# Expert shares carried in sorted rows, gathers that add to the residual, and products four heads at a time

## The chip, the core and the metric

The kernel runs on one core of a Trainium2 chip. The metric is the device time of one execution in microseconds (us), the median over several runs. The core has TensorE (PE; its weight loads are listed as PEld), VectorE (DVE), ScalarE (ACT) and GpSimd (POOL); SyncE (SP) issues most transfers, GpSimd issues the indirect ones. Each engine works through its own list of instructions in order, and semaphores order the engines among one another. SBUF is the memory the engines work in, PSUM the banks TensorE writes.

## What is computed

A decoder of two layers over x of 64 sequences of 64 positions and 256 channels, in float32; each sublayer normalises x and adds its result to it:

```python
# layer 0: gated linear attention of 16 heads, a recurrence over the context, experts
x = x + linear_attention(layernorm(x))
x = x + recurrence(k=layernorm(x), v=ctx, w, u)
h = layernorm(x)
top, index = top_2(h @ router_weight.T + router_bias)      # of 8 experts
share = softmax(top)                                       # two shares per token
x = x + sum over the two choices of share * expert(h)
# layer 1: attention D (windowed), cross attention E, attention F with a modulated MLP M
x = x + attention_D(layernorm(x))
q = (layernorm(x) @ Wq + bq), k, v = ctx @ Wk + bk, ctx @ Wv + bv    # 16 heads of 16
# scores between the HEADS of one token: 16 x 16 per token
x = x + softmax_g(q[h] . k[g]) v[g] @ Wo + bo
x = x + attention_F(...) ; x = x + mlp_M(...)
```

(The factor of the expert sum is taken into the shares: the kernel's expert outputs are twice the real ones, and its shares are halved.)

## The kernel before, in words

There are 4096 tokens, 32 tiles of 128 (one token per partition); x stays in SBUF as `x_sb` [128, 32, 256] from start to end. Three stages follow one another with a barrier between: linear attention (to 1480 us), `recurrence_and_experts` (to about 1935 us) and `layer_one`.

**Recurrence and router.** Eight blocks of four tiles go through ten steps (`STEPS`), with three blocks in work: one is being normalised and transposed, one scanned, one routed. On the routed block VectorE adds the recurrence's result (`residual`), takes statistics, and after TensorE's router product picks the two largest experts (`choose`, L1431 to L1441), ranks tokens within an expert and turns that into row numbers (`place`, L1458 to L1468). ScalarE computes the exponential of the gap of the two scores (`odds`, L1281). VectorE computes the two shares (`settle`, L1446 to L1451) in the next step, into `wts` [128, 32, 2]. GpSimd scatters the normalised rows `xh`, 256 floats each, to `sorted_rows` in HBM, grouped by expert: one indirect DMA per tile and choice (L1031), 64 in all, spread over the next step of its list. At the end VectorE makes a table of 39 tiles of 256 sorted rows, which expert each belongs to and where it starts (`tile_table`, L1487 to L1516), and SP fills the end of each expert's rows with zeros (L927) before any row is loaded.

**Experts.** For each of 39 tiles SP loads 256 rows (L945, four buffers `hs`) and 1 MB of gate and up weights (L951, three buffers), TensorE transposes the rows (L1198), multiplies with gate and up (L1211) and, after the activation, with down (L1225). ScalarE copies the transposes (`hT_out`), applies tanh, adds the bias to the up half (`up_out`) and copies the product (`aT_out`); VectorE makes the low parts (`rows_low`, L1560), the gate (L1571), L1577, the product (L1583) and the result (`result`, L1590, into two buffers `ys`), GpSimd clamps (L1072) and makes the low part (L1076). SP stores the results to `sorted_outs` (L956), in sorted order. In each engine's loop these pieces stand in an order that is written out by hand, several tiles apart.

**Layer one.** Here too the order is written by hand: `iterate` runs a counter i and calls, for each engine, a list of (stage, piece); a piece works on tile i - FIRST[stage]. FIRST is G=-2, Dn=-1, D=0, Dt=1, En=1, E=2, Et=3, F=4, Ft=5, M=7, Md=8, so eight to ten tiles are in work, each in another stage. What matters here:

- G, on GpSimd (`gather`): a copy of the tile's row numbers, two tiny instructions that act as fences (L1810 to L1814), and two indirect DMAs (L1816) that fetch the outputs of both choices into `got0` and `got1`.
- Dn, on VectorE (`combine`, L2221): x += share * got, twice; then the statistics of D.
- E: q to SBUF (L2080), then GpSimd multiplies (`products_qk`, L1797): 16 instructions, one per head, of 16 x 16 elements. VectorE sums four heads at a time (`et_scores`, L2295), subtracts the maximum (L2300, L2302), ScalarE exponentiates, VectorE divides (`et_weights`, L2307 to L2311). GpSimd multiplies the weights with the values (`products_av`, L1804), again 16 instructions, and VectorE sums (`et_values`, L2319). Both sets go through one buffer `prod`. TensorE transposes and projects the result (L1854, L1849) and VectorE adds it to x (`et_x`, L2325).
- F and M: `arguments` (L2266, L2269), `statistics` (L2232), `divide` (L2279, L2282), `f_x2lo` (L2341), `ft_gm_lo` (L2336), the MLP's silu (`m_hidden`, L2358, L2361), `m_x` (L2367). The first piece in GpSimd's list is F's power (L1787), so it stands behind the gathers of the iteration before.

TensorE's list in layer one is ("M", m_half(0)), D's and E's transposes, ..., ("F", f_zT), ("M", m_half(1)), ..., ("Md", m_down), ("Et", et_aT), ("Et", et_wo), ("F", f_s), and m_half waits until the silu has left the bank `GA`.

## Time and profile before

| | us |
|---|---|
| median of 3 runs | 3035.04 |
| lowest and highest | 3031.03, 3040.39 |
| the profiled execution, its own time | 3033.89 |
| its span in the trace | 3032.2 |
| TensorE busy | 2750.8 |
| VectorE busy | 2487.2 |
| ScalarE busy | 1954.2 |
| GpSimd busy | 2111.9 |

The profile is of one execution. The page gives busy time, a chain of waits followed back from the end and the costliest groups of instructions; the trace behind it gives every instruction with start and duration, and for idle time what ended it. A start is in us from the start of the span. "x16" is a run of sixteen alike instructions merged into one row. A duration includes the tail of a pipelined instruction, so the next can start before it is over; the steps from start to start tell what one costs in a row.

### The profile page before, as it was taken

How to read it: one execution, taken by the hardware profiler on the slowest of the kernel's cores; microseconds unless marked ns; L12 is line 12 of the kernel's file. 1: busy time of each engine (PE TensorE's matmuls, PEld its weight loads, DVE VectorE, ACT ScalarE, POOL GpSimd, SP SyncE). 2: the span in 40 equal slices, each digit the busy share in tenths (PEclk: the TensorE clock that was granted, in tenths of full speed). 3: DMA queues.
4: the chain of work that ended last, by engine and by line, in shares of the span. 5: the costliest groups of instructions: out<-in, count | busy, mean ns of one | idle time of the engine just before them, and what ended most of it. 6: DMA issues, size and time to landing. Idle time of an engine off the chain costs nothing. (4 is left out here: it accounts for less than half of the span.)

```text
span 3032.2 us, 68140 instructions
## 1 busy us (share of the span) xinstructions
PE 2750.8 (91%) x22096; PEld 2295.9 (76%) x22128; DVE 2487.2 (82%) x5452; ACT 1954.2 (64%) x4120; POOL 2111.9 (70%) x2651
## 2 busy tenths in 40 slices
PE   6999999999999999999788499667999999999978
PEld 3888888888888888888555299535777777777767
DVE  6888888888888888888599577468899898989863
ACT  5888878778787877878444155346666666666642
POOL 5897666666666666666468544369888989898870
PEclk9999999999999999999899699768999999999989
DMA  4555444444444444444444399600000000000000
GB/s 144 172 193 169 133 143 139 144 135 146 137 131 153 131 143 132 155 131 128 142 152 146 134 337 333 207 15 18 20 19 27 21 25 24 22 24 22 21 5 11
DMA packets 185881, 340.09 MB, mean 112 GB/s; under 512 B 40668, under 2 KB 104037, under 8 KB 178936
## 3 DMA queue, kind: packets, MB, share of 16 engines
q1 hardware_dynamic: 179448, 319.55, 32.6%
q0 software_dynamic: 6144, 16.79, 1.8%
q8 instruction: 169, 2.77, 0.4%
q14 instruction: 120, 0.98, 0.1%
HBM read 264.68 MB, written 63.19 MB: 108 GB/s over the span
## 5 line engine op out<-in xcount | busy, mean ns | idle before, releaser
L1804 POOL TENSOR_TENSOR l_prod<-l_sco,l_kv 128x256 f32<-128x256 f32 x512 | 369.5, 760 | 36.4 <-DVE l_sco L2311 36.4
L1797 POOL TENSOR_TENSOR l_prod<-l_q,l_kv 128x256 f32<-128x256 f32 x512 | 358.9, 743 | 47.3 <-DVE l_att L2319 47.3
L718 DVE SCALAR_TENSOR_TENSOR a_cq<-a_PQ,a_taps,a_cq 128x504 f32<-128x504 f32 (+2 forms) x384 | 281.7, 734 | 72.7 <-ACT a_cq L584 63.6
L718 DVE SCALAR_TENSOR_TENSOR a_ck<-a_PK,a_taps,a_ck 128x504 f32<-128x504 f32 (+2 forms) x384 | 280.6, 731 | 9.7 <-ACT a_ck L584 0.5
L342 POOL TENSOR_TENSOR a_tq<-a_cq,a_tq 128x512 f32<-128x512 f32 x128 | 165.9, 1296 | 131.2 <-ACT a_tq L590 131.1
L329 POOL TENSOR_TENSOR a_hrs<-a_hve,a_neghalf 128x8 f32<-128x8 f32 x128 | 209.6, 1638 | 25.7 <-DVE a_hve L735 25.2
L485 PE MATMUL a_Y<-a_wo,a_og_parts 128*128 128x256 f32 x1536 | 205.9, 284 | 5.0 <-POOL a_og_parts L336 5.0
L412 PEld LDWEIGHTS a_X<-a_wv,a_xb 128*128 128x128 f32 x1536 | 200.0, 188 | 12.1 <-issue 1.2
L342 POOL TENSOR_TENSOR a_tk<-a_ck,a_tk 128x512 f32<-128x512 f32 x128 | 163.6, 1278 | 62.8 <-ACT a_tk L590 62.8
L412 PE MATMUL a_PQ<-a_x_hi,a_wqk 128*128 (+1 forms) x512 | 194.1, 420 | 12.6 <-issue 11.9
L412 PE MATMUL a_X<-a_wv,a_xb 128*128 128x256 f32 x1536 | 204.2, 282 | 0.8 <-DMA a_xb<-a_x_lo 0.8
L603 ACT ACTIVATE a_hk<-a_PK,a_lncol 128x512 f32<-128x512 f32 x128 | 99.9, 781 | 154.6 <-PE a_PK L504 154.6
L485 PEld LDWEIGHTS a_Y<-a_wo,a_og_parts 128*128 128x128 f32 x1536 | 194.7, 192 | 6.0 <-issue 5.9
L597 ACT ACTIVATE a_nq<-a_TQ,a_hnb,a_hrs 128x128 f32<-128x128 f32 x512 | 192.5, 463 | 1.5 <-POOL a_hnb L332 1.0
L597 ACT ACTIVATE a_nk<-a_TK,a_hnb,a_hrs 128x128 f32<-128x128 f32 x512 | 191.5, 457 | 0.0
L412 PE MATMUL a_X<-a_x_hi,a_wg 128*128 (+1 forms) x512 | 183.5, 399 | 2.3 <-DVE a_og L743 2.3
L412 PE MATMUL a_PK<-a_x_hi,a_wqk 128*128 (+1 forms) x512 | 182.6, 397 | 0.0
L336 POOL TENSOR_TENSOR a_og_parts<-a_og,a_og_parts 128x512 fp32r<-128x512 f32 x128 | 166.7, 1302 | 17.6 <-ACT a_og_parts L610 17.6
L584 ACT ACTIVATE a_cq<-a_PQ,a_taps 128x512 f32<-128x512 f32 x128 | 99.9, 780 | 100.0 <-PE a_PQ L412 100.0
L325 POOL TENSOR_TENSOR a_hm<-a_hst 128x8 f32<-128x8 f32 x128 | 26.7, 209 | 191.9 <-DVE a_hst L724 191.9
L772 DVE TENSOR_TENSOR_SCAN a_em<-a_dr,a_dm 128x256 f32<-128x256 f32 x128 | 160.0, 1250 | 0.0
L2319 DVE TENSOR_REDUCE l_att<-l_prod 128x64 f32<-128x1024 f32 x128 | 151.7, 1206 | 8.2 <-POOL l_prod L1804 8.0
(398 smaller groups left out, 8380.6 us busy)
## 6 DMA issues: line engine op xcount, KB each, us to landing
a_wqk<-qk_parts SPq DMA_DIRECT2D x112, 512.0 KB, 3.4
m_wgu<-gate_up_parts SPq DMA_DIRECT2D x39, 1024.0 KB, 8.1
a_wv<-v_parts SPq DMA_DIRECT2D x56, 512.0 KB, 3.8
a_wg<-g_parts SPq DMA_DIRECT2D x112, 256.0 KB, 3.3
a_wo<-o_parts SPq DMA_DIRECT2D x112, 256.0 KB, 2.9
a_dr<-decays SPq DMA_DIRECT2D x256, 64.0 KB, 2.6
m_hs<-sorted_rows SPq DMA_DIRECT2D x39, 256.0 KB, 7.1
sorted_outs<-m_ys SPq DMA_DIRECT2D x39, 256.0 KB, 7.5
```

What stands on the lines that cost most here:

```text
L329: nc.gpsimd.tensor_tensor(out=hrs[q][:], in0=hve[q][:], in1=neghalf[:], op=ALU.pow).then_inc(s_hrstd, 1)
L336: nc.gpsimd.tensor_tensor(out=og_parts[q][:, 1, :], in0=og[q][:], in1=og_parts[q][:, 0, :].bitcast(F32), op=ALU.subtract).then_inc(og_lo, 1)
L342: nc.gpsimd.tensor_tensor(out=t[i][p][:], in0=c[i][p][:], in1=t[i][p][:], op=ALU.mult).then_inc(s_silu, 1)
L412: last = nc.tensor.matmul(out, lhs(i, k), rhs(j, k), start=at_pass == PASSES[0], stop=at_pass == PASSES[-1])
L485: last = nc.tensor.matmul(Y[:, j, :], og_parts[p][:, i, j * P:(j + 1) * P], wo[p][:, w, :], start=first and j % 2 == 0 and k == 0, stop=Tr ...
L584: nc.scalar.activation(c[i][p][:], PB[i][:], ACT.Identity, bias=taps[p][:, bias:bias + 1], scale=taps[p][:, tap + KW - 1:tap + KW]).then_i ...
L597: nc.scalar.activation(nrm[i][q][:, j, :], TB[i][:, j, :], ACT.Identity, bias=hnb[q][:, k:k + 1], scale=hrs[q][:, k:k + 1]).then_inc(s_nor ...
L718: nc.vector.scalar_tensor_tensor(out=acc, in0=src, scalar=taps[p][:, tap + k:tap + k + 1], in1=acc, op0=ALU.mult, op1=ALU.add).then_inc(s_ ...
L772: nc.vector.tensor_tensor_scan(out=flat(em[q]), data0=flat(dr[q]), data1=flat(dm[q]), initial=0.0, op0=ALU.mult, op1=ALU.add).then_inc(s_e ...
L1797: nc.gpsimd.tensor_tensor(out=prod[:, h], in0=qv[:, h:h + 1, :].to_broadcast([P, H, HD]), in1=kk, op=ALU.mult).then_inc(S("E_pqk"), 1)
L1804: nc.gpsimd.tensor_tensor(out=prod[:, h], in0=sco[:, h:h + 1, :].to_broadcast([P, HD, H]), in1=vv, op=ALU.mult).then_inc(S("E_pav"), 1)
L2319: nc.vector.reduce_sum(att[:].rearrange("p (h d) -> p h d", d=HD)[:, 4 * k:4 * k + 4, :], prod[:, 4 * k:4 * k + 4], axis=AX).then_inc(S("E ...
```

## The change

Rows that are scattered are three floats wider: they carry the number of the token's first expert, the share of the second choice (`SHARE`) and what the first has more (`MORE`). In the expert stage VectorE compares the first number with the tile's expert and so gets each row's share (`first_choice`, `shares`), and ScalarE multiplies the result with it (`weigh`) before it is stored; `ys` has three buffers and the store comes one step later. The buffer `wts` is gone. In layer one the gathers add straight to `x_sb` in the DMA, the first choice in a new stage G0 (FIRST -3) and the second in G, which waits for the first; `combine`, the copies and the fences are gone. The products of cross attention are issued for four heads at a time.

```diff
...
     I2 = 2 * D
+    FIRST_EXPERT, MORE, SHARE, WIDE = D, D + 1, D + 2, D + 3
...
-        zeros, ends = sb("zeros", [P, D]), sb("ends", [P, E], mybir.dt.int32)
+        zeros, ends = sb("zeros", [P, WIDE]), sb("ends", [P, E], mybir.dt.int32)
...
-        xh = some(2, "xh", [P, BT, D])
+        xh, w0 = some(2, "xh", [P, BT, WIDE]), sb("w0", [P, BT])
...
-            hs = own_some(4, "hs", [P, 2, D])
+            hs = own_some(4, "hs", [P, 2, WIDE])
+            pick, w_of = own_some(2, "pick", [P, 2]), own_some(8, "w_of", [P, 2])
...
+            aT, ys = own_some(2, "aT", [P, 2, DC, ROWS], F32R), own_some(3, "ys", [P, 2, D])
...
-            LOADS, STORES = 4, 2
+            LOADS, STORES = 4, 3
...
-                             zeros[:].unsqueeze(1).to_broadcast([P, 2, D])).then_inc(S("filled"), 16)
+                             zeros[:].unsqueeze(1).to_broadcast([P, 2, WIDE])).then_inc(S("filled"), 16)
...
@@ -941,6 +943,7 @@
                 def load(i):
                     if i >= LOADS:
                         sp.wait_ge(S("x_hT"), i - LOADS + 1)
+                        sp.wait_ge(S("x_share"), i - LOADS + 1)
                     at = sp.value_load(where_i[0:1, i:i + 1], min_val=0, max_val=E * ROOM)
                     sp.dma_start(hs[i % LOADS][:], rows[bass.ds(at, ROWS), :].rearrange("(h p) d -> p h d", p=P)).then_inc(S(f"x_in{i % LOADS}"), 16)
...
                 def store(i):
-                    sp.wait_ge(S("x_y"), i + 1)
+                    sp.wait_ge(S("x_ys"), 2 * i + 2)
...
                         load_weights(i)
-                for i in range(-3, N + 1):
-                    if i >= 1:
-                        store(i - 1)
+                for i in range(-3, N + 2):
+                    if i >= 2:
...
                 def scatter(b, part=slice(0, 2 * BT)):
                     pool.wait_ge(S("slot"), b + 1)
                     pool.wait_ge(S("xh"), 4 * b + 4)
+                    pool.wait_ge(S("carried"), 3 * b + 3)
                     for j, k in [divmod(n, 2) for n in range(2 * BT)][part]:
...
-                        nc.scalar.activation(out[:, j, :], x_sb[:, b * BT + j, :], ACT.Identity, bias=nm[k][:, j:j + 1],
+                        nc.scalar.activation(out[:, j, 0:D], x_sb[:, b * BT + j, :], ACT.Identity, bias=nm[k][:, j:j + 1],
...
-                for i in range(-3, N):
+                def weigh(i):
+                    act.wait_ge(S("x_share"), i + 1)
+                    act.wait_ge(S("x_y"), i + 1)
+                    for h in range(2):
+                        nc.scalar.activation(ys[i % STORES][:, h, :], ys[i % STORES][:, h, :], ACT.Identity,
+                                             scale=w_of[i % 8][:, h:h + 1]).then_inc(S("x_ys"), 1)
+
+                for i in range(-3, N + 1):
                     if i + 3 < N:
                         hT_out(i + 3)
                     if 0 <= i + 1 < N:
@@ -1367,6 +1378,8 @@
                     if 0 <= i + 2 < N:
                         tanh(i + 2)
                         up_out(i + 2)
+                    if i >= 1:
+                        weigh(i - 1)
...
                     nc.vector.tensor_copy(ixf[:, b * BT:(b + 1) * BT, :], ix8[:, :, 0:2]).then_inc(S("ixf"), 1)
+                    nc.vector.tensor_copy(xh[b % 2][:, :, FIRST_EXPERT], ix8[:, :, 0]).then_inc(S("carried"), 1)
...
                     dve.wait_ge(S("odds"), b + 1)
                     nc.vector.tensor_scalar(te[:, 2, :], te[:, 1, :], 1.0, 2.0, ALU.add, ALU.mult).then_inc(S("sum2"), 1)
                     dve.wait_ge(S("sum2"), b + 1)
-                    own_w = wts[:, b * BT:(b + 1) * BT, :]
-                    nc.vector.reciprocal(own_w[:, :, 0], te[:, 2, :]).then_inc(S("w0"), 1)
+                    nc.vector.reciprocal(w0[:], te[:, 2, :]).then_inc(S("w0"), 1)
                     dve.wait_ge(S("w0"), b + 1)
-                    nc.vector.tensor_tensor(out=own_w[:, :, 1], in0=own_w[:, :, 0], in1=te[:, 1, :], op=ALU.mult).then_inc(S("w1"), 1)
+                    share, more = xh[b % 2][:, :, SHARE], xh[b % 2][:, :, MORE]
+                    nc.vector.tensor_tensor(out=share, in0=w0[:], in1=te[:, 1, :], op=ALU.mult).then_inc(S("carried"), 1)
+                    dve.wait_ge(S("carried"), 3 * b + 2)
+                    nc.vector.tensor_tensor(out=more, in0=w0[:], in1=share, op=ALU.subtract).then_inc(S("carried"), 1)
...
                         weights_low(y)
-                    if r:
-                        settle(r - 1)
...
                     if r is not None:
                         place(r)
+                        settle(r)
                 tile_table()
-                settle(BLOCKS - 1)
...
+                def first_choice(i):
+                    dve.wait_ge(S(f"x_in{i % LOADS}"), 16 * (i // LOADS + 1))
+                    row = hs[i % LOADS]
+                    nc.vector.scalar_tensor_tensor(out=pick[i % 2][:], in0=row[:, :, FIRST_EXPERT], scalar=who[:, i:i + 1],
+                                                   in1=row[:, :, MORE], op0=ALU.is_equal, op1=ALU.mult).then_inc(S("x_pick"), 1)
+
+                def shares(i):
+                    dve.wait_ge(S("x_pick"), i + 1)
+                    if i >= 8:
+                        dve.wait_ge(S("x_ys"), 2 * (i - 8) + 2)
+                    nc.vector.tensor_tensor(out=w_of[i % 8][:], in0=pick[i % 2][:], in1=hs[i % LOADS][:, :, SHARE],
+                                            op=ALU.add).then_inc(S("x_share"), 1)
...
                     if i + 3 < N:
+                        first_choice(i + 3)
                         rows_low(i + 3)
+                        shares(i + 3)
...
-    FIRST = dict(G=-2, Dn=-1, D=0, Dt=1, En=1, E=2, Et=3, F=4, Ft=5, M=7, Md=8)
+    FIRST = dict(G0=-3, G=-2, Dn=-1, D=0, Dt=1, En=1, E=2, Et=3, F=4, Ft=5, M=7, Md=8)
...
-        got = [sb(f"got{k}", [P, D]) for k in range(2)]
-        of_tile, ready = sb("of_tile", [P, 2], mybir.dt.uint32), sb("ready", [P, 1])
...
-                    sp.wait_ge(S("E_pav"), H * (t - 2))
+                    sp.wait_ge(S("E_pav"), 4 * (t - 2))
...
@@ -1793,32 +1820,31 @@
                 wait_if(pool, S("E_att"), 4 * t)
                 qv = q[:].rearrange("p (h d) -> p h d", d=HD)
                 kk = kv[t % 3][:, 0, :].rearrange("p (g d) -> p g d", d=HD)
-                for h in range(H):
-                    nc.gpsimd.tensor_tensor(out=prod[:, h], in0=qv[:, h:h + 1, :].to_broadcast([P, H, HD]), in1=kk,
-                                            op=ALU.mult).then_inc(S("E_pqk"), 1)
+                for k in range(4):
+                    heads = slice(4 * k, 4 * k + 4)
+                    nc.gpsimd.tensor_tensor(out=prod[:, heads], in0=qv[:, heads, :].unsqueeze(2).to_broadcast([P, 4, H, HD]),
+                                            in1=kk.unsqueeze(1).to_broadcast([P, 4, H, HD]), op=ALU.mult).then_inc(S("E_pqk"), 1)
             def products_av(t):
                 pool.wait_ge(S("E_w"), t + 1)
                 vv = kv[t % 3][:, 1, :].rearrange("p (d g) -> p d g", d=HD)
-                for h in range(H):
-                    nc.gpsimd.tensor_tensor(out=prod[:, h], in0=sco[:, h:h + 1, :].to_broadcast([P, HD, H]), in1=vv,
-                                            op=ALU.mult).then_inc(S("E_pav"), 1)
-
-            def gather(t):
-                wait_if(pool, S("G_ready"), 2 * t)
-                wait_if(pool, S("G_x"), 2 * t)
-                nc.gpsimd.tensor_tensor(out=ready[:], in0=neghalf[:, 0:1], in1=neghalf[:, 0:1], op=ALU.mult).then_inc(S("G_ready"), 1)
-                nc.gpsimd.tensor_copy(of_tile[:], slots[:, tile(t), :].rearrange("p t k -> p (t k)")).then_inc(S("G_at"), 1)
-                pool.wait_ge(S("G_ready"), 2 * t + 1)
-                pool.wait_ge(S("G_at"), t + 1)
-                nc.gpsimd.tensor_tensor(out=ready[:], in0=neghalf[:, 0:1], in1=neghalf[:, 0:1], op=ALU.mult).then_inc(S("G_ready"), 1)
-                for k in range(2):
-                    nc.gpsimd.indirect_dma_start(got[k][:], None, outs[:, :],
-                                                 bass.IndirectOffsetOnAxis(ap=of_tile[:, k:k + 1], axis=0)).then_inc(S(f"G_in{k}"), 16)
+                for k in range(4):
+                    heads = slice(4 * k, 4 * k + 4)
+                    nc.gpsimd.tensor_tensor(out=prod[:, heads], in0=sco[:, heads, :].unsqueeze(2).to_broadcast([P, 4, HD, H]),
+                                            in1=vv.unsqueeze(1).to_broadcast([P, 4, HD, H]), op=ALU.mult).then_inc(S("E_pav"), 1)
+
+            def gather(k):
+
+                def piece(t):
+                    if k:
+                        pool.wait_ge(S("G_in0"), 16 * t + 16)
+                    nc.gpsimd.indirect_dma_start(x_sb[:, t, :], None, outs[:, :], bass.IndirectOffsetOnAxis(ap=slots[:, t, k:k + 1], axis=0),
+                                                 compute_op=ALU.add).then_inc(S(f"G_in{k}"), 16)
+                return piece
             pool.wait_ge(S("masked"), 4)
             iterate(pool, [("F", power("F", 2)), ("Et", products_av), ("Dn", power("D", 1)), ("En", power("E", 1)), ("E", products_qk),
-                           ("G", gather)])
+                           ("G", gather(1)), ("G0", gather(0))])
...
-
-            def combine(t):
-                for k in range(2):
-                    dve.wait_ge(S(f"G_in{k}"), 16 * t + 16)
-                    if k:
-                        dve.wait_ge(S("G_x"), 2 * t + 1)
-                    nc.vector.scalar_tensor_tensor(out=row(t), in0=got[k][:], scalar=wts[:, tile(t), k:k + 1].rearrange("p t k -> p (t k)"),
-                                                   in1=row(t), op0=ALU.mult, op1=ALU.add).then_inc(S("G_x"), 1)
...
-                    wait_if(dve, S("E_pav"), H * t)
-                    dve.wait_ge(S("E_pqk"), H * t + 4 * k + 4)
+                    wait_if(dve, S("E_pav"), 4 * t)
+                    dve.wait_ge(S("E_pqk"), 4 * t + k + 1)
...
                     wait_if(dve, S("E_aTp"), t)
-                    dve.wait_ge(S("E_pav"), H * t + 4 * k + 4)
+                    dve.wait_ge(S("E_pav"), 4 * t + k + 1)
...
-                          ("M", m_hidden(0)), ("D", d_rope), ("Dn", combine), ("Et", et_values(0)), ("Ft", divide("F", MI)),
-                          ("Dn", statistics("D", "G_x", 2)), ("F", f_x2lo), ("Dt", d_x), ("M", m_hidden(1)),
+                          ("M", m_hidden(0)), ("D", d_rope), ("Et", et_values(0)), ("Ft", divide("F", MI)),
+                          ("Dn", statistics("D", "G_in1", 16)), ("F", f_x2lo), ("Dt", d_x), ("M", m_hidden(1)),
...
-        wts = ctx.enter_context(nc.sbuf_tensor("wts", [P, TILES, 2], F32))
-        rows = nc.dram_tensor("sorted_rows", (8 * (TOK + 2 * P) + 2 * P, D), F32, kind="Internal").ap()
+        rows = nc.dram_tensor("sorted_rows", (8 * (TOK + 2 * P) + 2 * P, D + 3), F32, kind="Internal").ap()
...
```

## Rows read from the trace of the kernel before

**Rows 1.** The page's chain of waits, shares by engine.
```profile
DVE 11%; POOL 10%; PE 8%; issue 6%; ACT 1%; DVEq 0%; POOLq 0%; ACTq 0%
```

**Rows 2.** Busy time by stretch: PE, PEld, DVE, ACT, POOL; clock, DMA share, GB/s.
```profile
1750.00:1930.00 180.00, 177.95 (x1504) 177.75 (x1502) 134.35 (x228) 97.81 (x189) 87.79 (x114) 1.00 0.94 314
2300.00:2830.00 530.00, 498.15 (x4384) 400.18 (x4401) 479.11 (x984) 329.04 (x824) 475.77 (x708) 1.00 0.08 24
```

**Rows 3.** Timeline, VectorE, a tile: start, us, operation, count, idle before.
```profile
2515.25 0.42 DVE L2325 TENSOR_TENSOR x_sb<-l_EB,x_sb 128x256 f32<-128x256 f32 x1 [1.60 <-PE l_EB L1849]
2524.80 0.42 DVE L2282 TENSOR_TENSOR l_oD<-l_EB,l_recD 128x256 f32<-128x256 f32 x1
2526.22 0.68 DVE L2358 SCALAR_TENSOR_TENSOR l_hid<-l_hid,l_GA 128x512 f32<-128x512 f32 x1
2529.32 1.72 DVE L2221 SCALAR_TENSOR_TENSOR x_sb<-l_got,wts,x_sb 128x256 f32<-128x256 f32 x2
2545.24 0.42 DVE L2325 TENSOR_TENSOR x_sb<-l_EB,x_sb 128x256 f32<-128x256 f32 x1 [1.58 <-PE l_EB L1849]
```

**Rows 4.** Timeline, TensorE in the same tile.
```profile
2527.04 0.95 PE L2019 MATMUL l_GA<-l_x,l_win 128*128 128x256 f32 x6
```

**Rows 5.** Timeline, GpSimd's products in the first and the last tiles.
```profile
1998.18 10.94 POOL L1797 TENSOR_TENSOR l_prod<-l_q,l_kv 128x256 f32<-128x256 f32 x16
2013.13 11.28 POOL L1804 TENSOR_TENSOR l_prod<-l_sco,l_kv 128x256 f32<-128x256 f32 x16 [0.65 <-DVE l_sco L2311]
2025.83 16.01 POOL L1797 TENSOR_TENSOR l_prod<-l_q,l_kv 128x256 f32<-128x256 f32 x16 [0.38 <-DVE l_att L2319]
2058.95 10.93 POOL L1797 TENSOR_TENSOR l_prod<-l_q,l_kv 128x256 f32<-128x256 f32 x16 [0.47 <-DVE l_att L2319]
2088.63 11.01 POOL L1797 TENSOR_TENSOR l_prod<-l_q,l_kv 128x256 f32<-128x256 f32 x16 [2.12 <-DVE l_att L2319]
...
2900.04 11.02 POOL L1797 TENSOR_TENSOR l_prod<-l_q,l_kv 128x256 f32<-128x256 f32 x16 [2.01 <-DVE l_att L2319]
2931.40 11.00 POOL L1797 TENSOR_TENSOR l_prod<-l_q,l_kv 128x256 f32<-128x256 f32 x16 [5.41 <-DVE l_att L2319]
2946.37 11.20 POOL L1804 TENSOR_TENSOR l_prod<-l_sco,l_kv 128x256 f32<-128x256 f32 x16 [3.31 <-DVE l_sco L2311]
```

**Rows 6.** Groups of GpSimd in the recurrence: busy us, mean ns, idle before.
```profile
L1025 POOL TENSOR_TENSOR m_fv<-m_fk,m_vt 128x1024 f32<-128x1024 f32 x8 | 18.8, 2351 | 0.2 <-ACT m_fk L1271 0.2
L1018 POOL TENSOR_TENSOR m_ev<-m_eh,m_vt 128x1024 f32<-128x1024 f32 x8 | 17.4, 2178 | 10.7 <-ACT m_eh L1266 10.7
```

**Rows 7.** The gathers' tile: time from issue to landing.
```profile
DMA to landing us min/median/max: 2.7/2.8/7.3
```

**Rows 8.** Timeline, VectorE at the start of layer one.
```profile
1948.56 0.48 DVE L2221 SCALAR_TENSOR_TENSOR x_sb<-l_got,wts,x_sb 128x256 f32<-128x256 f32 x1 [0.84 <-DMA l_got<-sorted_outs,l_of_tile]
```

**Rows 9.** Transposes of the experts' rows: ns min/median/max, first and last start.
```profile
L1198 PE MATMUL m_TV<-ident,m_hs x156: 270/272/476, 1738.2 to 1917.6; 128*128 128x128 f32 x156
```

**Rows 10.** Timeline, VectorE's gate of two expert tiles.
```profile
1751.34 0.87 DVE L1571 TENSOR_SCALAR m_gp<-m_TK,m_bias_of 128x256 f32<-128x256 f32 x2
1755.61 0.87 DVE L1571 TENSOR_SCALAR m_gp<-m_TK,m_bias_of 128x256 f32<-128x256 f32 x2
```

**Rows 11.** Timeline of the recurrence: a scatter on GpSimd, the last slot numbers.
```profile
1628.57 0.98 POOL L1031 DMA_INDIRECT sorted_rows<-m_xh,m_sent_to  x1 [3.02 <-DVE m_sent_to L1468]
...
1721.20 0.17 DVE L1468 CAST m_sent_to<-m_row_of 128x8 uint32<-128x8 f32 x1
```

**Rows 12.** Timeline, ScalarE, four normalisations in a row.
```profile
1656.61 2.07 ACT L1258 ACTIVATE m_xn<-x_sb,m_nm,m_rs 128x256 f32<-128x256 f32 x4 [2.93 <-POOL m_nm L1004]
```

**Rows 13.** DMA queues from 1760 to 1920 us: packets, MB, share.
```profile
q1 hardware_dynamic: 22718, 51.95, 97.4%
```

**Rows 14.** Timeline, VectorE, a four-element instruction of the recurrence.
```profile
1622.98 2.60 DVE L1431 TENSOR_TENSOR m_te<-m_mx 128x4 f32<-128x4 f32 x1
```

**Rows 15.** One line's instructions: duration ns min/median/max, first and last start.
```profile
L2341 DVE TENSOR_TENSOR l_x<-l_x2f,l_x x32: 412/416/2843, 2051.0 to 2975.9; 128x256 fp32r<-128x256 f32 x32
```

## Prediction of the time, made before the changed kernel ran

> **What bounds the kernel now.** I read the page first, for its chain of waits, then the windows for the three stretches that the change touches, then the timelines of one tile of layer one, engine by engine. The chain of waits is shared out over VectorE, GpSimd and TensorE [rows 1], so no engine bounds alone. In the steady part of layer one TensorE is busy 498.15 of 530 us, VectorE 479.11 and GpSimd 475.77, at the full granted clock (1.00, 2.4 GHz) [rows 2]. There the order of the queues decides, and the timelines show the loop. A period is the step between two residual additions of cross attention on VectorE (L2325): 2515.25 to 2545.24, 29.99 us [rows 3]. Both start after an idle gap of 1.60 and 1.58 us that ended with TensorE's product (L1849), so VectorE has slack there. From 2515.25 VectorE works without a gap to the silu (L2358, ends 2526.90), 11.65 us; D's division (L2282) at 2524.80 is in it [rows 3]. TensorE's next gate product (L2019) starts at 2527.04, 0.14 us after the silu frees its bank [rows 4], and TensorE then runs through its in-order list to the product that VectorE waits for at 2545.24 [rows 3], 18.2 us. 11.65 + 0.14 + 18.2 = 29.99: this loop, half VectorE and half TensorE, sets the period. The two weighted additions of the expert outputs (L2221, 1.72 us at 2529.32) [rows 3] are behind the silu and ahead of the gap, in the part of VectorE's list with 1.6 us of slack.
>
> At the ends of layer one it is otherwise. In the first three tiles GpSimd runs its two sets of 16 products nearly back to back, with idle gaps of 0.65, 0.38 and 0.47 us, and the loop is 2025.83 - 1998.18 = 27.65, then 33.12, then 29.68 us, the last of them ending in a wait of 2.12 us for VectorE. In the last tiles the sets stand alone on the path with only softmax and reductions between [rows 5].
>
> **The products.** Sets of 16 instructions of 256 elements take 10.94 and 11.28 us where little disturbs them [rows 5], some 0.69 each, 2.77 us for four heads. One instruction of 1024 elements on GpSimd takes 2.351 or 2.178 us [rows 6]. So a set of four costs 8.7 to 9.4 us; I take the middle, 9.06, a saving of 1.9 and 2.2 us per set. These rows have plain operands, not ones spread over heads; bounds are no saving and the full 8.7. VectorE's reductions work on four heads at a time already and wait for the same data.
> - First tiles: loop 1 saves both sets, 4.1 us. Loop 2 as much, 4.2 (its set of 16.01 us [rows 5] holds a stall beside VectorE's split of weights that stays). Loop 3, which ends in VectorE's wait, some 2.5, and the next 0.8. Together -11.6 (-6 to -14).
> - Steady tiles: neither set is in the loop above. 0 (-1 to +1).
> - Last tiles: the sets at 2931.40 and 2946.37 are wholly on the path: 11.00 + 11.20 - 18.12 = 4.1. The one at 2900.04 holds back F's power behind it in the queue: 2.0. Of the loop before I count 1.5 and of the values' set in between 1.0. Together -8.6 (-4 to -11).
>
> **The gathers.** Both additions leave VectorE: 1.72 us per tile less, but in the slack, so the gap at L2325 grows from 1.60 to 3.3 us and the period stays. GpSimd loses three small instructions and keeps two gathers. In a steady tile the second gather is a whole period behind the first, so its wait is met, and its landing has over 10 us before D's statistics. An accumulating gather isn't in the trace; a plain one lands in 2.7 to 7.3 us [rows 7]. At the start of layer one it costs: now both first gathers fly together beside the weight loads, and the second addition runs at 1948.56 for 0.48 us [rows 8]. After, the second is issued only when the first has landed. One landing more is 2.8 to 7.3 us [rows 7]; I take 6, as the weight loads fill the queues, less 2 for the addition, the three small instructions and the spacing of the two: +4 (+2 to +7). Behind that wait on GpSimd stands D's power, which needs the same data anyway.
>
> **The experts.** The transposes of 39 tiles start from 1738.2 to 1917.6 [rows 9], 4.72 us a tile, with TensorE busy 177.95 of 180 us [rows 2]: it is the bound. Added per tile are two VectorE instructions on 2 elements, in the loop gate, tanh, up, clamp, product, rows, gate. Where TensorE doesn't hold it that loop takes 1755.61 - 1751.34 = 4.27 us [rows 10]; two small ones (an estimate of 0.17 us each, the length of the small cast [rows 11]) make it 4.6, under 4.72. ScalarE gains two activations on 256 elements; four such take 2.07 [rows 12], so 1.04 a tile, and it is busy 54% [rows 2]. They fit where it now waits for the transposes. SP's store now waits for the scaling, with the loads of rows and weights queued behind it; it comes one step later and has a third buffer, so by then the scaling is done. The loads wait in addition for the shares, which follow the transposes at once. Rows of 1036 bytes are 1.2% more of a sixth of the bytes, and the hardware queue is at 97.4% [rows 13], still under. With so little room I add 2 us for jitter (0 to 8), and 1.1 for the last tile's scaling, ahead of its store.
>
> **The recurrence.** Shares are settled right after the slots, and each scatter waits for them. The settling waits for ScalarE's exponential of the same step, which is a router's step old by then; behind it on VectorE stand the next step's statistics. GpSimd already waits for the slot numbers (3.02 us before a scatter [rows 11]), so a scatter and the power queued behind it come some 0.4 us later, and VectorE has two more instructions of some 0.17 us. 0.35 x 8 = 2.8. After the last slots (cast at 1721.20 [rows 11]) the settling stands ahead of the table that the loads wait for: 0.7. Together +3.5 (+1 to +6).
>
> **Sum.** 3.5 + 2 + 1.1 + 4 - 11.6 + 0 - 8.6 = -9.6 us. The profiled execution took 3033.89 us (span 3032.2), so 3024.3; the median of the runs is 1.15 above it: 3025.5. All low ends together give -22, all high ends +13. A measurement of this kernel can tell 0.3%, 9.1 us, from no change: the border is 3026, so this forecast is as likely just over it as under.
>
> **Rivals.**
> - Each tile gets shorter by what VectorE loses. For it: VectorE leads the chain of waits with 11% [rows 1] and is busy 90%. Against it: the gap of 1.60 us in every period [rows 3]. If the 1.72 us count in the 27 tiles from the fourth to the end of D: 3025.5 - 46 = 2979.
> - The products don't get shorter, as the operands spread over four heads cost per element what they cost now. Nothing in the trace shows the form. The 20.2 us of both ends go, but 3 for the small instructions ahead of F's power: 3025.5 + 17 = 3043.
> - Slower, by longer waits between VectorE and GpSimd. A VectorE instruction of 4 elements took 2.60 us at 1622.98 [rows 14], in the stretch where GpSimd runs instructions of 1024 elements, and L2341 took up to 2.84, with a median of 0.42 [rows 15]. Both read two SBUF tensors. L2341 and L2336 are such, both between silu and L2325, beside products that now last 2.3 us. Two full waits are 4.7 us against 3.3 of slack; as all tiles keep the same phase it is all of them or none. It decides from 3.3 us on; at 1.0 over in 27 tiles: 3025.5 + 27 = 3052. Against it: the median of L2341 shows no wait at all in most of its 32 runs [rows 15].
> - Wide rows are moved as if they had 2048 bytes. A sixth of 4.7 us more DMA time a tile, 0.78, less 0.12 of room, in 39 tiles: 3025.5 + 26 = 3051. Nothing speaks for it but that no row of the trace has such a size with such starts.
>
> On the third of these the Trainium skill speaks against the change. Its page "SBUF — State Buffer", section "SBUF: two separate sides", says that VectorE with two SBUF inputs and GpSimd take a shared port pair for a whole instruction, and the loser is blocked until the end. By that rule the wait grows with the length of a product, fourfold. The trace agrees in the row at 1622.98; the 2.84 us beside products of 0.69 is longer than the rule gives.
>
> **How the numbers follow.** Forecast 0.64, tiles shorter 0.15, products no shorter 0.08, port waits 0.08, wide rows 0.05. The predicted time is the forecast's, 3025. All of its ends together give 3013 and 3048, which hardly meet; with the spread of the runs themselves (3031.03 to 3040.39) its own range is 3008 to 3043. Up to 3052 the three others come in, and the first rival (0.15) and the tails stay out; the low end gets 2 us more for a period that shrinks a little. Over 0.3% faster: half of the forecast and the first rival, 0.32 + 0.15 = 0.47. Slower by over 0.3%: port waits 0.08, wide rows 0.05, 0.03 from the products' case and 0.02 from the forecast's tail, 0.18. Within: the rest, 0.35.
>
> **What would show it.** In the timeline of GpSimd a set of four near 9.1 us; the step between two L2325 (now a later line) still 30.0 us, with the idle gap before it at 3.3; no VectorE line for gathers, D's statistics of the first tile near 1953; the experts' transposes still 4.72 us apart; the first three loops of products shorter by 4, 4 and 2.5 us. A period under 29.5 or over 30.3 us would make the prediction wrong, as 27 tiles multiply it; so would experts' tiles 0.3 us longer, or a landing of an accumulating gather of over 10 us.

## The result and the profile after

The changed kernel takes 3049.89 us (median of 8 runs, 3046.16 to 3055.54), the kernel before 3032.44 us (8 runs): ratio 1.0061, 95% interval 1.0047 to 1.0075. It is 0.6% slower, where I had forecast 0.3% faster. The profiled execution has a span of 3053.8 us against 3032.2. This is how the 21.6 us between the two spans lie over the stages, read from first and last starts that are rounded to 0.1 us:

| stretch | before | after | diff. | predicted |
|---|---|---|---|---|
| linear attention, to the recurrence's first statistics | 1487.7 | 1491.4 | +3.7 | not touched |
| recurrence, to the last slot numbers | 233.5 | 245.8 | +12.3 | +2.8 |
| to the first load of sorted rows | 14.3 | 18.2 | +3.9 | +0.7 |
| to the first transposes of the experts | 2.7 | 2.8 | +0.1 | |
| first to last transposes | 179.4 | 178.1 | -1.3 | +2 |
| to the start of layer one | 18.9 | 20.6 | +1.7 | +1.1 |
| to D's first statistics | 12.6 | 19.4 | +6.8 | +4 |
| to the first residual addition of cross attention | 80.4 | 76.6 | -3.8 | with the fill |
| 28 steps between such additions | 845.7 | 848.6 | +2.9 | fill -11.6, steady 0 |
| to the end | 157.0 | 152.3 | -4.7 | -8.6 |

Linear attention has the same code in both, and its end lies between 1486.4 and 1496.9 us in the traces of this study; its 3.7 us are the spread between executions. The rest, 17.9 us, agrees with the medians (17.5 us apart). The recurrence varies too: with the changed kernel's code it took 245.9 to 249.5 us in five traces (after, r_only, early_low, late_loads, silu_first), with the old code 232.1 to 234.9 us in five (before, p_only, g_only, p_pairs, before_silu_first). The two groups lie 11 us apart or more; smaller differences of this stretch, read from one trace each, are weak.

The timeline of VectorE in a steady tile of layer one, after (start, us, operation, count, idle before):

```profile
2751.71 0.42 DVE L2343 TENSOR_TENSOR x_sb<-l_EB,x_sb 128x256 f32<-128x256 f32 x1
2762.68 0.68 DVE L2376 SCALAR_TENSOR_TENSOR l_hid<-l_hid,l_GA 128x512 f32<-128x512 f32 x1
2767.99 0.26 DVE L2297 RECIPROCAL l_recF<-l_MI 128x16 f32<-128x16 f32 x1 [0.99 <-PE l_MI L1907]
2769.51 0.65 DVE L2359 TENSOR_TENSOR l_x<-l_x2f,l_x 128x256 fp32r<-128x256 f32 x1
2778.85 2.45 DVE L2354 TENSOR_TENSOR l_gm<-l_gmT,l_gm 16x128 fp32r<-16x128 f32 x1
2781.68 0.42 DVE L2343 TENSOR_TENSOR x_sb<-l_EB,x_sb 128x256 f32<-128x256 f32 x1
```

The step is 2781.68 - 2751.71 = 29.97 us, as before [rows 3], and the two weighted additions are gone. But the gap ahead of the residual addition (now L2343) is gone too, where I expected 3.3 us: the modulation's low part (L2354, before L2336, 0.59 us) takes 2.45 us, the low part of x2 (L2359) 0.65 instead of 0.42 [rows 15], and VectorE waits 0.99 us for TensorE at L2297: 1.86 + 0.23 + 0.99 = 3.1 us of the 3.3. Where an instruction of VectorE or GpSimd lasts longer beside work of the other one, I call the excess a port wait, after the rule that the prediction cites; the trace shows the duration and what runs beside it, not the port.

GpSimd's products in the first and last tiles, which answer to [rows 5]:

```profile
2025.38 9.23 POOL L1825 TENSOR_TENSOR l_prod<-l_q,l_kv 128x1024 f32<-128x1024 f32 x4
2049.28 13.36 POOL L1825 TENSOR_TENSOR l_prod<-l_q,l_kv 128x1024 f32<-128x1024 f32 x4 [0.40 <-DVE l_att L2337]
2071.99 9.42 POOL L1833 TENSOR_TENSOR l_prod<-l_sco,l_kv 128x1024 f32<-128x1024 f32 x4 [4.18 <-DVE l_sco L2329]
2083.67 9.26 POOL L1825 TENSOR_TENSOR l_prod<-l_q,l_kv 128x1024 f32<-128x1024 f32 x4 [1.25 <-DVE l_att L2337]
...
2955.22 9.31 POOL L1825 TENSOR_TENSOR l_prod<-l_q,l_kv 128x1024 f32<-128x1024 f32 x4 [5.41 <-DVE l_att L2337]
2968.54 9.30 POOL L1833 TENSOR_TENSOR l_prod<-l_sco,l_kv 128x1024 f32<-128x1024 f32 x4 [3.35 <-DVE l_sco L2329]
```

An undisturbed set takes 9.2 to 9.3 us (9.06 was predicted; 10.94 to 11.28 before). Loop 1 is 2049.28 - 2025.38 = 23.9 us, 3.75 less; loops 3 and 4 take 28.8 and 31.1 us (29.7 and 30.7 before). But loop 2 is 34.4 us, 1.3 more: one set takes 13.36 us, and in the same stretch VectorE's split of the weights takes longer. First VectorE before, then after:

```profile
2029.83 2.28 DVE L2348 TENSOR_TENSOR l_win<-l_hid,l_win 128x2048 fp32r<-128x2048 f32 x1
2032.04 2.80 DVE L2348 TENSOR_TENSOR l_wup<-l_hid,l_wup 128x2048 fp32r<-128x2048 f32 x1
2034.87 1.63 DVE L2350 TENSOR_TENSOR l_fb<-l_fb 16x1024 fp32r<-16x1024 f32 x1
```

```profile
2053.26 2.81 DVE L2366 TENSOR_TENSOR l_win<-l_hid,l_win 128x2048 fp32r<-128x2048 f32 x1
2056.00 4.42 DVE L2366 TENSOR_TENSOR l_wup<-l_hid,l_wup 128x2048 fp32r<-128x2048 f32 x1
2060.45 3.27 DVE L2368 TENSOR_TENSOR l_fb<-l_fb 16x1024 fp32r<-16x1024 f32 x1
```

10.5 us against 6.7: both engines take longer beside one another. The length of the products does it: in p_only, which changes the products alone, the three rows take 10.6 us, in g_only and r_only, with the old products, 6.7. The start of layer one on GpSimd and VectorE, after:

```profile
1959.29 1.68 POOL L1841 DMA_INDIRECT x_sb<-sorted_outs,slots  x1 [0.28 <-POOL l_cmask L1808]
1966.93 1.56 POOL L1841 DMA_INDIRECT x_sb<-sorted_outs,slots  x1 [5.96 <-DMA x_sb<-sorted_outs,slots]
```

```profile
1976.28 0.43 DVE L2250 BATCH_NORM_STATS2 l_stD<-x_sb 128x6 f32<-128x256 f32 x1
```

The second gather is issued 7.6 us after the first, when that has landed, and D's statistics start 9.35 us later. In the recurrence GpSimd waits for the share (`m_xh`, L1467), and some of its scatters and powers take longer. A step after, GpSimd and then VectorE:

```profile
1610.10 0.99 POOL L1035 DMA_INDIRECT sorted_rows<-m_xh,m_sent_to  x1 [1.54 <-DVE m_xh L1467]
1611.39 1.86 POOL L1035 DMA_INDIRECT sorted_rows<-m_xh,m_sent_to  x1 [0.30 <-issue]
1613.28 1.04 POOL L1005 TENSOR_TENSOR m_rs<-m_ve,m_neghalf 128x4 f32<-128x4 f32 x1
...
1614.55 2.35 POOL L1028 TENSOR_TENSOR m_fv<-m_fk,m_vt 128x1024 f32<-128x1024 f32 x1
1617.06 3.01 POOL L1035 DMA_INDIRECT sorted_rows<-m_xh,m_sent_to  x1 [0.17 <-issue]
1620.38 0.97 POOL L1035 DMA_INDIRECT sorted_rows<-m_xh,m_sent_to  x1 [0.30 <-issue]
1621.38 2.19 POOL L1005 TENSOR_TENSOR m_rs<-m_ve,m_neghalf 128x4 f32<-128x4 f32 x1
```

```profile
1611.20 1.22 DVE L1488 TENSOR_TENSOR m_wgu<-m_raw_gu,m_wgu 128x1024 fp32r<-128x1024 f32 x1
...
1615.51 1.42 DVE L1395 TENSOR_SCALAR m_ve<-m_mv 128x4 f32<-128x4 f32 x1
...
1616.91 2.31 DVE L1412 TENSOR_TENSOR_SCAN m_qp<-m_keep,m_eh 128x1040 f32<-128x1040 f32 x1
```

The ordinary price of a scatter is 0.98 us [rows 11]; at 1611.39 it takes 1.86 and at 1617.06 3.01, while VectorE subtracts two SBUF tensors of 1024 elements (L1488) and scans two of 1040 (L1412). The Trainium skill, page "SBUF — State Buffer", section "SBUF: two separate sides", describes that GpSimd can't write the descriptors of a DMA while VectorE holds the shared ports, and it names a VectorE copy in a two-port mode. The trace shows longer issues in these two rows, beside a subtraction and a scan, which that passage doesn't name.

The other direction is in the same rows: L1395, four elements that the power needs as its argument, takes 1.42 us beside GpSimd's product (L1028). Its 16 instructions take 10.5 us in the changed kernel and 3.3 us before. It reads one SBUF tensor, so the waits are not of two-operand instructions alone.

### The profile page after: what moved, and what is told of

Its sections match the earlier page's. It is cut to its first block and busy times, and to the rows that moved or that the text cites. A ratio compares the mean times of both kernels' runs of the same rounds, so it can differ in the third digit from the quotient of the medians.

```text
span 3053.8 us, 67425 instructions
## 1 busy us (share of the span) xinstructions
PE 2751.4 (90%) x22128; PEld 2297.4 (75%) x22128; DVE 2520.5 (83%) x5482; ACT 1981.5 (65%) x4198; POOL 2018.0 (66%) x1787
## 3 DMA queue, kind: packets, MB, share of 16 engines
q1 hardware_dynamic: 179448, 319.70, 32.2%
q0 software_dynamic: 12288, 16.88, 2.8%
## 5 line engine op out<-in xcount | busy, mean ns | idle before, releaser
L1825 POOL TENSOR_TENSOR l_prod<-l_q,l_kv 128x1024 f32<-128x1024 f32 x128 | 303.1, 2400 | 96.8 <-DVE l_att L2337 96.8
L1833 POOL TENSOR_TENSOR l_prod<-l_sco,l_kv 128x1024 f32<-128x1024 f32 x128 | 303.3, 2407 | 86.2 <-DVE l_sco L2329 86.2
```

The costliest lines, as they stand in the source:

```text
L1825: nc.gpsimd.tensor_tensor(out=prod[:, heads], in0=qv[:, heads, :].unsqueeze(2).to_broadcast([P, 4, H, HD]), in1=kk.unsqueeze(1).to_broadca ...
L1833: nc.gpsimd.tensor_tensor(out=prod[:, heads], in0=sco[:, heads, :].unsqueeze(2).to_broadcast([P, 4, HD, H]), in1=vv.unsqueeze(1).to_broadc ...
```

## The experiments

**Each part alone.** `p_only` is the kernel before with this edit, for both sets of products (and the semaphore counts that go with it):

```diff
-                for h in range(H):
-                    nc.gpsimd.tensor_tensor(out=prod[:, h], in0=qv[:, h:h + 1, :].to_broadcast([P, H, HD]), in1=kk,
+                for k in range(4):
+                    heads = slice(4 * k, 4 * k + 4)
+                    nc.gpsimd.tensor_tensor(out=prod[:, heads], in0=qv[:, heads, :].unsqueeze(2).to_broadcast([P, 4, H, HD]),
+                                            in1=kk.unsqueeze(1).to_broadcast([P, 4, H, HD]), op=ALU.mult).then_inc(S("E_pqk"), 1)
```

> The kernel before with the products four heads at a time and nothing else. Theory (two loops share the 30 us of a tile of layer one; waits between VectorE and GpSimd fill VectorE's slack): the subtraction for the modulation's low part takes 2.45 us instead of 0.59 and the low part of x2 some 0.25 more, 2.1 us together against a gap of 1.6 us that the combine leaves, so the step between two residual additions of cross attention grows from 29.99 to some 30.5 us, about +13 us over the steady tiles; the first loop of products is shorter by 3.7 us and the last tiles by 4 to 5. In all 3032 + 13 - 5 = 3040 us. Rival 1 (TensorE alone sets the step): step 29.98, total 3025 to 3028 us. Rival 2 (the longer waits come only through the gathers that write to x in place): the subtraction stays at 0.6 us, step 29.98, total 3020 to 3024 us.

Measured: 3117.72 us, ratio 1.0289 (1.0257 to 1.0322), 85 us slower; steps of 32.9 to 35.1 us. All three expectations were wrong. VectorE and then TensorE in a tile:

```profile
2574.31 4.55 DVE L2223 SCALAR_TENSOR_TENSOR x_sb<-l_got,wts,x_sb 128x256 f32<-128x256 f32 x2
2590.42 2.46 DVE L2338 TENSOR_TENSOR l_gm<-l_gmT,l_gm 16x128 fp32r<-16x128 f32 x1
```

```profile
2580.83 0.41 PE L1856 MATMUL l_MI<-ident,l_oF 128*128 128x128 f32 x2 [0.53 <-DVE l_oF L2284]
2582.22 0.66 PE L1844 MATMUL l_EB<-l_dwv,l_xTD 128*128 128x64 f32 x4 [0.98 <-DVE x_sb L2290]
```

I had counted the low part's wait (2.46 us, as expected) and forgotten the combine, whose operands lie in SBUF too: 4.55 us instead of 1.72. 2.83 + 1.87 us more go beyond the slack, and TensorE now waits inside its list, for F's division and D's addition to x. The changed kernel has the same products without the combine, and its step is 29.97 us.

`g_only` is the kernel before with the adding gathers (diff as in the change; it leaves the shares out of the sum).

> The kernel before with the adding gathers and without VectorE's combine; the shares are left out of the sum. Theory: the step in the steady tiles stays at 29.98 us, with the gap ahead of the residual addition at 3.2 us or more; the start of layer one is 6.8 us later, for the second gather waits for the first and each adding gather takes longer to land (3.8 against 2.8 us); total 3032 + 7 = 3039 us. Rival (each tile gets shorter by what VectorE loses, 1.7 us): step 28.3 us, total 2993 us. Rival (the start costs nothing beside the weight loads): total 3032 us.

Measured: 3063.85 us, ratio 1.0102 (1.0059 to 1.0146), 25 us over the theory's 3039. 18 of the 31 steps are 29.98 to 30.00 us. The gap ahead of the addition is 1.6 us, not the 3.2 expected; VectorE spends another 1.06 us a tile waiting for TensorE at the reciprocal of F (16.9 us in 16 tiles), and the low part of x2 takes 0.85 us on average instead of 0.42. So a tile does not get shorter by what VectorE loses. D's statistics come 21.4 us behind the start of layer one, 8.8 more than before. Four tiles take 34.3 to 37.4 us, and the 28 steps of the table 863.0 against 845.7 us; in the first of them there is this row, beside products of 0.69 us:

```profile
2063.83 6.33 DVE L2330 TENSOR_TENSOR l_x<-l_x2f,l_x 128x256 fp32r<-128x256 f32 x1
```

`r_only` is the changed kernel with the gathers, combine (factor 1) and products of before.

> The changed kernel's recurrence and experts (wide rows, shares settled before the scatter, scaling on ScalarE), with gathers, combine (its factor now 1) and products of layer one as before. Theory: the recurrence takes 12 us more and the first load of rows comes 4 us later, the experts add about 1; layer one as before; total 3032 + 17 = 3049 us. Rival (the stages up to layer one differ only from run to run): total 3032 to 3037 us.

Measured: 3056.07 us, ratio 1.0068 (1.0042 to 1.0094): in its trace recurrence 246.0 us, first load 18.4 us behind it, layer one as before. Against the forecast of +17 us it is +24 in the median, and +17.2 in the span. This part alone is as slow as the whole change.

**The recurrence.** `settle_aside` settles at the old place into a buffer of its own, and the scatters don't wait for it; the rows carry zero shares, so the experts' outputs are left out of x. `settle_unwaited` is the same with the settling at the new place.

```diff
-                    pool.wait_ge(S("carried"), 3 * b + 3)
+                    pool.wait_ge(S("carried"), b + 1)
...
-                    share, more = xh[b % 2][:, :, SHARE], xh[b % 2][:, :, MORE]
+                    share, more = aside[:, 0, :], aside[:, 1, :]
```

> The changed kernel, but the shares are settled where they were before, one step late, into a buffer of their own, and the scatters don't wait for them: the rows carry zeros as shares, so the experts' outputs are left out of x. Rows stay 1036 bytes. Theory (the place of the settling costs the recurrence its 2.6 us a step: it pushes the second scatter into VectorE's 1.2 us split of weights and the power behind both): ten steps take 233 to 235 us from the first statistics to the last slot numbers instead of 245.8; the first load of rows after the last scatter still comes 7.7 us later instead of 4.8. Rival (the wide rows slow the scatters on GpSimd): 243 to 246 us, whatever the place of the settling.

> As settle_aside (shares into a buffer of their own, the experts' outputs left out of x), but VectorE settles them at the new place, right behind the slot numbers; the scatters still don't wait for it. It tells VectorE's order from the scatters' wait. Theory (it is the scatters' wait, with the powers queued behind it): the stretch from the first statistics to the last slot numbers takes 233 to 236 us, as in settle_aside (232.5). Rival (it is VectorE's order: statistics, split and residual come later, and into other waits): 241 to 246 us.

The groups of the slot numbers, in settle_aside, settle_unwaited and the changed kernel; the recurrence ends with the last start in each:

```profile
L1486 DVE CAST m_sent_to<-m_row_of x8: 171/171/2595, 1546.1 to 1720.6; 128x8 uint32<-128x8 f32 x8
```

```profile
L1486 DVE CAST m_sent_to<-m_row_of x8: 170/171/2594, 1547.9 to 1730.0; 128x8 uint32<-128x8 f32 x8
```

```profile
L1484 DVE CAST m_sent_to<-m_row_of x8: 171/171/2608, 1549.3 to 1737.2; 128x8 uint32<-128x8 f32 x8
```

From first statistics at 1488.1, 1490.0 and 1491.4 these are 232.5, 240.0 and 245.8 us. The wide rows cost nothing here (233.5 us before); the place of the settling costs it all. By these traces it is 7.5 us by VectorE's order alone (the theory had said none) and 5.8 us by the scatters' wait. The sum is clear of the spread of some 3 us of this stretch, the split is less sure. The power's argument (L1395 in the changed kernel) fits the second part: 4.1 us in settle_unwaited, 10.5 in the changed kernel, 6.4 more; that this wait is the cause no run shows. The one run of settle_aside took 3032.47 us, that of settle_unwaited 3039.62. `powers_first` and `before_powers_first` issue one scatter ahead of the first power and three behind the second:

```diff
-                        scatter(r - 1, slice(0, 2))
+                        scatter(r - 1, slice(0, 1))
...
-                    if r:
-                        scatter(r - 1, slice(2, 4))
                     if r is not None:
                         power(1, r)
+                    if r:
+                        scatter(r - 1, slice(1, 4))
```

> The changed kernel, with one scatter ahead of the first power of a step instead of two, and three behind the second power instead of two ahead of it. Theory (what the settling cost in the recurrence is GpSimd's scatters standing ahead of the powers on the loop from statistics to router): VectorE's wait for the router's product (2.9 us a step) goes, the step falls from 29.2 to some 26.5 us, and the stretch from the first statistics to the last slot numbers from 245.8 to some 230 us; total 3050 - 16 = 3034 us. Rival (VectorE itself sets the step, the order of scatters is hidden): 245 us and 3050 us.

> The same move of the scatters in the kernel before. Theory: VectorE waits 2.5 us a step for the router's product there too, so the stretch falls from 233.5 to some 221 us; total 3032 - 12 = 3020 us. Rival (without the settling the powers were on time): 233 us, 3032 us.

Measured: 3040.54 us (1.0018, 1.0001 to 1.0036) and 3039.5 us (1.0021, 1.0005 to 1.0037). The theories had said 3034 and 3020 us. The recurrence falls from 245.8 to 237.7 us in the one, half of the theory, and from 233.5 to 232.5 in the other, which is within its spread. The power, freed from the scatters, meets VectorE's scan:

```profile
1610.65 2.95 POOL L1005 TENSOR_TENSOR m_rs<-m_ve,m_neghalf 128x4 f32<-128x4 f32 x1 [0.17 <-DVE m_ng L1398]
```

**The loop in layer one.** `early_low` moves ("Ft", ft_gm_lo) in VectorE's list ahead of ("D", arguments("D")).

> The changed kernel, with the subtraction for the modulation's low part directly behind the last sum of cross attention's values, where GpSimd starts no product yet. It then takes 0.3 to 0.6 us instead of 2.45. Theory (the mixed loop of the silu on VectorE and TensorE's list sets the 29.97 us, and the wait only fills slack): step still 29.9 to 30.0 us, a gap of some 2 us again ahead of the residual addition, total 3047 to 3050 us. Rival (VectorE's own list sets the step in the changed kernel): step 28.1 us, total 3050 - 45 = 3005 us.

Measured: 3059.37 us (1.0081, 1.0055 to 1.0107), step 30.23 us. In steady tiles the subtraction still takes 2.14 us on average (0.28 in two of 16, 2.4 in the others), so the run hardly makes the change that it was to test. Nothing of the rival's 28.1 us is seen; why the step grew by 0.26 us is not shown. `silu_first` and `before_silu_first`:

```diff
-                          ("Et", et_scores(1)), ("Et", et_scores(3)), ("Et", et_shift), ("Dt", divide("D", EB)), ("Et", et_weights),
-                          ("M", m_hidden(0)), ("D", d_rope)
+                          ("Et", et_scores(1)), ("Et", et_scores(3)), ("Dt", divide("D", EB)), ("Et", et_shift), ("M", m_hidden(0)),
+                          ("Et", et_weights), ("D", d_rope)
```

> The changed kernel, with D's division ahead of the subtraction of the maximum, and the first half of the silu ahead of the weights, in VectorE's list. TensorE waits 0.75 us a tile for D's division and 0.13 us for the silu. Theory (a loop through these two sets the 29.97 us, in which the combine never lay): step 29.2 to 29.4 us, total 3050 - 17 = 3033 us. Rival (VectorE's whole list with its waits for GpSimd is as long as that loop, and the weights now come a microsecond later to GpSimd): step 29.97 us or more, total 3050 to 3060 us.

> The same move in the kernel before. Theory: there VectorE has 1.6 us of slack too, step 29.2 to 29.4 us, total 3033 - 17 = 3016 us. Rival (GpSimd's longer sets of 11 us, each started later, become the bound): step 30 us or more, total 3033 to 3045 us.

Measured: 3072.03 us (1.0114, 1.0088 to 1.0141) with steps of 31.02 us, and 3042.79 us (1.0014, 0.9999 to 1.0030) with steps of 30.2 us. The rivals hold in the step; silu_first's total is 12 us over its rival's 3060. TensorE in silu_first:

```profile
2560.06 0.27 PE L1873 MATMUL l_EB<-l_ebq,l_ones 3*128 3x256 bf16 x1 [0.54 <-DVE l_oD L2300]
2562.36 0.44 PE L1880 MATMUL l_MI<-ident,l_xnF 128*128 128x128 f32 x2 [0.98 <-ACT l_xnF L2091]
```

The wait for the division shrinks from 0.75 to 0.54 us, and two matmuls later ScalarE's normalised x (0.98 us) is late instead. L2359 now meets a product in most tiles of silu_first (2.04 us on average, 0.77 in the changed kernel).

**The start.** `late_loads` puts two waits, for the first tile's gathers, ahead of SP's load of F's output weights.

> The changed kernel, where the loads of layer one's weights from the output projection of F onward wait for the first tile's two gathers. Theory (the two gathers land in 7.6 and 9.4 us because the queues are full of weights): each lands in some 4 us, D's first statistics come 11 us behind the start of layer one instead of 19.4, total 3050 - 8 = 3042 us. Rival (an adding gather takes this long at the start whatever else flies, or the late weights hold up the first tiles): no gain or a loss, 3050 to 3056 us.

Measured: 3048.37 us (1.0048, 1.0027 to 1.0068). D's statistics come 10.9 us behind the start, as expected: the first two gathers land in 4.25 and 3.82 us instead of 7.38 and 9.19. But the total misses the 3042 us of the theory. The recurrence took 248.7 us in this trace, and three steps take 32.1 to 32.2 us where the changed kernel has one. The late loads need not be the reason: powers_first has three such steps without them, two_moves one with them. The row behind such a step, in the changed kernel:

```profile
2587.94 2.60 DVE L2359 TENSOR_TENSOR l_x<-l_x2f,l_x 128x256 fp32r<-128x256 f32 x1
```

A full wait for a product (0.42 + 2.2) is a step of 32.2 instead of 29.97 us.

`all_three` joins late_loads and silu_first with this edit, and settles the shares at the old place (those lines are not shown); the scatters of a step come behind both powers:

```diff
                 for f, y, r in STEPS:
-                    if r:
-                        scatter(r - 1, slice(0, 2))
...
-                    if r:
-                        scatter(r - 1, slice(2, 4))
                     if r is not None:
                         power(1, r)
+                    if r:
+                        scatter(r - 1, slice(0, 4))
```

> The changed kernel with three moves: shares settled one step late as before, the first four scatters of a step behind both powers, so that they find them settled; the later weight loads of layer one behind the first tile's gathers; and the order of silu_first. Theory: the stretch from the first statistics to the last slot numbers 233 to 237 us instead of 245.8, D's first statistics 11 us behind the start of layer one instead of 19.4, step as silu_first shows. If that is 29.3 us: 3050 - 11 - 6 - 17 = 3016 us; if it stays at 30: 3033 us. Rival for the recurrence (the first powers were not held by the scatters): 245 us.

Measured: 3053.14 us (1.0060, 1.0038 to 1.0081). The recurrence takes 232.6 us and the start 11.1; both as expected, and the order of silu_first gives all of it back (steps of 31.02 us).

**Length of a product, and the mended change.** `p_pairs` is p_only with two heads at a time. `two_moves` is all_three without silu_first, and `two_moves_pairs` the same with two heads at a time.

> The kernel before with the products two heads at a time (512 elements, 1.2 us each), nothing else. Theory (VectorE, with two operands in SBUF, waits for the end of the running product): the low part of the modulation takes up to 1.3 us (0.59 with one head, 2.25 with four), a combine some 1.2 us (0.80; 2.22), together some 1.4 us more a tile, against 1.6 us of slack: the step stays at 30.0 to 30.3 us instead of 33.0 with four heads; total 3025 to 3040 us. Rival (operands spread over several heads slow VectorE whatever their length): the same 2.2 us as with four heads, and a step near 33 us.

> all_three without the order of silu_first: the changed kernel with shares settled one step late behind which the scatters come, and the later weight loads behind the first gathers. Theory: recurrence 232.6 us as in all_three, D's statistics 11 us behind the start of layer one, step 29.97 us again: 3053 less 27 steps of 1.05 us, 3025 us, 8 us under the kernel before; where three tiles of 32.2 us come in, as in late_loads, 3031 us. Rival (the change costs something in layer one beyond start and recurrence): 3035 us or more.

> two_moves with the products two heads at a time. Theory: the waits of VectorE halve (low part of the modulation 1.3 us instead of 2.45), no tile takes 32 us any more, the split of the weights in the first tiles takes less than 10.5 us; the sets take 10 us instead of 9.3, which no steady tile shows and the last three tiles show by 2 us: 2 to 6 us under two_moves. Rival (the waits lie in slack everywhere): as two_moves or up to 3 us above it, for the longer sets.

VectorE's groups in steady tiles (busy us, mean ns), first p_only, then p_pairs:

```profile
L2223 DVE SCALAR_TENSOR_TENSOR x_sb<-l_got,wts,x_sb 128x256 f32<-128x256 f32 x30 | 66.5, 2216 | 1.7
L2338 DVE TENSOR_TENSOR l_gm<-l_gmT,l_gm 16x128 fp32r<-16x128 f32 x15 | 33.8, 2254 | 0.5
L2343 DVE TENSOR_TENSOR l_x<-l_x2f,l_x 128x256 fp32r<-128x256 f32 x15 | 6.2, 415 | 0.0
```

```profile
L2223 DVE SCALAR_TENSOR_TENSOR x_sb<-l_got,wts,x_sb 128x256 f32<-128x256 f32 x32 | 38.7, 1208 | 1.8
L2343 DVE TENSOR_TENSOR l_x<-l_x2f,l_x 128x256 fp32r<-128x256 f32 x16 | 20.9, 1307 | 0.0
L2338 DVE TENSOR_TENSOR l_gm<-l_gmT,l_gm 16x128 fp32r<-16x128 f32 x17 | 5.1, 303 | 0.5
```

One addition of the combine takes 0.80, 1.21 and 2.22 us on average beside products of 0.69, 1.25 and 2.33 us: the wait grows with the product. That is the case of the rule that the prediction had cited against the change. Which instruction waits is a matter of phase (L2338 in the one, L2343 in the other). p_pairs took 3042.2 us in its one run, its step 30.83 us instead of the 30.0 to 30.3 expected: VectorE's instructions take 1.4 us more, as expected, but TensorE now waits for D's addition to x (0.57 us a tile, none before) while a gap of 1.0 us is still there behind it. The slack ahead of that addition is smaller than the gap at the end of the list.

two_moves: 3034.32 us (12 runs), ratio 0.9986 (0.9971 to 1.0001). two_moves_pairs: 3034.55 us, ratio 0.9985 (0.9969 to 1.0001). By these ratios both are 0.75% under the changed kernel, and not told apart from the kernel before. The theory holds for recurrence (233.5 us), start (11.0 us) and step (29.97 us, one of 32.2); its total, 3025 to 3031 us, was not reached. The first load still comes 17.5 us behind the recurrence (14.3 before): the wide zero rows are still there. Pairs neither end the long steps (two of 31.7) nor bring a gain.

## Why the prediction was wrong

The forecast of -9.6 and the +17.9 of the profiles are 27.5 us apart: 12.7 in the recurrence with the first load, 10.7 in the first tiles and the steps behind them, 3.9 in the last tiles, 2.8 in the gathers, less 2.6 in the experts.

- **Recurrence: the step that failed.** "so a scatter and the power queued behind it come some 0.4 us later, and VectorE has two more instructions of some 0.17 us. 0.35 x 8 = 2.8." Measured 12.3 us, 1.5 a step. I priced the added instructions by their length and took the rest of the step as rigid. settle_aside, settle_unwaited and all_three show that the place of the settling is the whole of it. The rows above show how a shift of 0.4 us can cost more: scatters, powers and L1395 come to lie beside longer work of the other engine. How much of the 12.3 us is such waiting stays open: in all_three the 16 powers take 33.6 us, more than the changed kernel's 25.4, and its recurrence still takes 232.6 us.
- **First load: failed, by a rival that I had priced on the wrong side.** I had asked what wide rows cost when they are read; they cost when they are written. The zero rows are written before the loads may start. Their landing (min/median/max), before and then after:

```profile
DMA to landing us min/median/max: 2.4/2.7/2.8
```

```profile
DMA to landing us min/median/max: 2.9/4.9/6.0
```

  SP waited 2.4 us for them before and 5.5 after. 3.1 of the 3.9 us lie here, 0.8 in the settling ahead of the table (0.7 predicted). settle_aside, with wide rows and the old place of the settling, has the same late zero rows and its first load 17.0 us behind the recurrence. Reading them is not slower (6.0 us to landing, 7.1 before), and the experts' tiles did not get longer, against the rival.
- **Experts:** right in the main. 4.69 us a tile, +0.4 us for the transposes and the end of the stage against +3.1.
- **Gathers:** mechanism right, size too small (+6.8 for +4). The first two landings took 7.38 and 9.19 us, where I had taken 6 for one more; late_loads shows that the weights in the queues do this. In the median an adding gather lands in 3.8 us (2.8 for a plain one) and takes GpSimd 1.6 us to issue instead of 1.0.
- **Steady tiles: right for a reason only half seen.** The step stayed (29.97), and g_only refutes that a tile gets shorter by VectorE's 1.72 us. But the slack was needed: 2.1 us of port waits came in, as the rival said they could, under its point of 3.3 us. One tile went over: 2.2 us. Neither early_low nor silu_first shortened the step, so which loop sets the 29.97 us stays open: the prediction led it over the silu, for which TensorE hardly waits (0.14 us), but ahead of that TensorE waits some 0.8 us a tile for D's division.
- **Fill (the first tiles of layer one): failed.** -11.6 predicted; -3.8 up to the first addition, then +1.5 in the next nine steps. Loop 1 saved 3.75 us of the 4.1 worked out. Loops 2 to 4 were to save 7.5 us and together took 0.8 more. Loop 2 was taken to save 4.2 us although VectorE's split of the weights stood in it; I took its stall to stay as it was, and with the longer products it grew by 3.8 us.
- **Last tiles:** right in kind, mis-sized. Two sets on the path save 1.7 and 1.9 us; for the sets before them I had counted 4.5 us more, and together they gave about 1: -4.7 for -8.6.

In sum the saving of the products was counted at 20 us and came to 5.6, and the loss before it at 10.6 and came to 23.5.

## What to carry to other kernels

Where instructions of VectorE and GpSimd wait for one another, the price of one depends on the length of what runs on the other engine. So before making GpSimd's instructions longer, look for VectorE's SBUF work beside them, and count on it taking longer. A small instruction added ahead of a queue is priced by what the queue then collides with: put it where its result is still in time, as two_moves does, which gave the 12 us back. Slack is read at the next waiter of an instruction, not at the next idle gap of its engine.

## What was not expected of the hardware

- A VectorE subtraction of 256 elements took 6.33 us (g_only) beside products of 0.69 us: the wait can last over several products, not one as by the rule that the prediction cites.
- Four elements' power on GpSimd took 2.95 us instead of 1.04 beside a scan on VectorE; the wait goes both ways.
- Four elements on VectorE with one SBUF operand (L1395) took 1.42 us instead of 0.17 beside a GpSimd product.
- Writes of 1036-byte rows are slower: from the first issue of zero rows to the last landing it is 15.2 us against 12.0 with rows of 1024 bytes, for the same eight transfers beside eight scatters. The Trainium skill, page "DMA: Bandwidth & Descriptors", section "How a descriptor splits into AXI transactions", counts extra beats for transfers that start off a 256-byte boundary, and says so of reads; here the reads did not land later and the writes did. The cause on the write side stays open.
- Adding in the DMA doubled the packets of the software queue (6144 to 12288 for the same 128 transfers).
- What of the 7.5 us of VectorE's order in the recurrence is port waits and what is plain order was not taken apart.
